# Edge stage of a graph network on one Trainium2 core: the lower parts of the normalised rows computed on GpSimd, the first sums waiting for them by fifths, and the remainders of the later edge weights moved to later rounds

## The chip, the core and the metric

The kernel runs on 1 core of one Trainium2 chip. The core has five engines with a queue each: TensorE (PE, matmuls; PEld are its weight loads), VectorE (DVE), ScalarE (ACT), GpSimd (POOL) and SyncE (SP, which only starts DMAs here). They meet through semaphores. The metric is the device time of one execution in microseconds: 2258.76 us before the change, the median of 3 runs (2257.27 to 2259.66).

## The reference, cut to what matters

Two layers act on x of 3125 nodes by 256 features with 100000 edges sorted by destination. The stage that is changed computes the first neighbour sum and, in the same pass, the matrix of edge weights that the second layer needs:

```
xn    = layernorm(x)
neigh = segment_sum(xn[src], dst, n)          # the edge stage: sums of gathered rows
h     = (1 + eps) * xn + neigh                # and, beside it, A[src, dst] += edge_weight
h     = relu(h @ W1 + b1) @ W2 + b2           # two dense layers, run inside the edge stage
h     = batchnorm(h) * gamma + beta
x     = x + h + attention(xn)                 # then experts, a second graph layer, experts
```

## The kernel before, in words

The nodes are padded to T = 25 tiles of 128. The edges lie in 1564 windows; four windows make an octet (391 of them), two octets a batch of 8 windows. For a batch, VectorE writes three tiles in `hots_dve` (L1001, L1002, L1006): one-hot rows of the keys, one-hot rows of the low bits (`lo`), and the one-hot keys times the three bf16 parts of the edge weight. TensorE multiplies them in `hots_pe` (L1027, L1029, L1032) into a bank for each octet (banks 0 to 3 in turn). ScalarE copies each bank out twice in `hots_act` (L1048): the counts to `CNT` (in `WB`) and the weights to `AWB` (in `X`). The one-hot tiles have two buffers: VectorE's batch n waits until TensorE is through with batch n-2 (`win`). A bank is used again when ScalarE has emptied it (`wev`).

Eight batches make a round, b = 0 to 24, which fills 128 columns of the counts. In round b+1 TensorE also forms the sums of round b (`sums_pe`, L1088): 25 tiles of counts times the normalised rows, each as an upper part `xnh` and a lower part `xnl` (fp32r words), in eight pieces i = 0 to 7 of 3 or 4 tiles. Batches are done in pairs, so TensorE's order in a round is batches 0 and 1, pieces 0 and 1, batches 2 and 3, pieces 2 and 3, and so on. From round 3 the dense layers (L1130, L1140) run in between as well.

The two parts of the rows are made in round 0. ScalarE rounds the rows of five tiles (a fifth, 1280 columns) into `xnh` (L1200) behind its batches 1 to 5. VectorE subtracts, `xnl = xn - xnh`, in place over `XN` (L1226), behind its batches 3 to 7. The first piece of sums (b = 1, i = 0) waits for all five lower parts.

The weights of the edges are turned into columns by TensorE ahead of the stage and split into three bf16 parts: VectorE's remainders (`first_rest_dve` L432, `second_rest_dve` L440) and ScalarE's casts (`highs_act`, `mids_act` L436, `lows_act` L444). There are four groups f of 512 windows (the last has 28). Groups 0 and 1 are done before the stage, groups 2 and 3 in rounds 1 and 2. Group f is first read in round 8 f. The order of each engine is written out by hand: `count_dve`, `count_act`, `count_pe` and `count_pool` are loops over rounds and i. On GpSimd, `count_pool` reads a flag and opens the semaphore `gate`, for which `sums_dve` (L1113) of round 2 waits; from there until its first gather at 649 us GpSimd has nothing to do.

Of the kernel before, what the change touches and what calls it, by code (L numbers as in the profile page):

```python
# [5 lines left out]
F32 = mybir.dt.float32  # L6
# [3 lines left out]
ALU = mybir.AluOpType  # L10
# [6 lines left out]
T = 25  # L17
# [54 lines left out]
def program(nc, ctx, a, out):  # L72
    at, sems = {}, {}

    def S(name):
        if name not in sems:
            sems[name] = ctx.enter_context(nc.semaphore(name))
        return sems[name]
# [233 lines left out]
    def degrees_pool(e):  # L312
        e.wait_ge(S("fold"), 2 * WG)
        e.wait_ge(S("good"), 1)
        e.tensor_scalar(deg2, deg2, goodc, None, ALU.mult).then_inc(S("degrees"), 1)
        e.wait_ge(S("degrees"), 1)
        e.dma_start(DEG.rearrange("(g p r) -> p g r", g=WG, r=2), deg2).then_inc(S("deg_out"), 16)
# [39 lines left out]
    def twice(v):  # L357
        return v.unsqueeze(2).to_broadcast([128, v.shape[1], 2])
# [61 lines left out]
    def dve_step(f, k):  # L420
        return FILLS + 4 * (f // 2) + 2 * k + f % 2 + 1

    def act_step(f, k):
        return FILLS + 6 * (f // 2) + 2 * k + f % 2 + 1

    def rest_of(f):
        o = windows_of(f)
        return left[f][:, 0:o.stop - o.start]
# [5 lines left out]
    def mids_act(e, f):  # L434
        e.wait_ge(S("key16"), dve_step(f, 0))
        e.copy(parts2[f][:, :, 1, :], twice(rest_of(f))).then_inc(S("lo16"), 1)  # L436

    def second_rest_dve(e, f):
        e.wait_ge(S("lo16"), act_step(f, 1))
        e.tensor_tensor(rest_of(f), rest_of(f), parts2[f][:, :, 1, 0], ALU.subtract).then_inc(S("key16"), 1)  # L440

    def lows_act(e, f):
        e.wait_ge(S("key16"), dve_step(f, 1))
        e.copy(parts2[f][:, :, 2, :], twice(rest_of(f))).then_inc(S("lo16"), 1)  # L444
# [522 lines left out]
    xnh, xnl = hr_, XNr  # L967
# [82 lines left out]
    def octets_to(b):  # L1050
        return min(16 * (b + 1), OCTETS)
# [20 lines left out]
    def fifth(g):  # L1072
        return slice(g * 5 * D, (g + 1) * 5 * D)

    xn_all = XN[:, :, :].rearrange("p t d -> p (t d)")

    def sums_pe(e, b, i):
        bk = B[4 + b % 2]
        if i == 0:
            e.wait_ge(S("cev"), octets_to(b))  # L1080
            if b == 0:
                e.wait_ge(S("xmix"), PAIRS)
                e.wait_ge(S("xnl"), 5)
            if b >= 2:
                e.wait_ge(S("gadd"), b - 1)
        for h in range(T * i // 8, T * (i + 1) // 8):
            for x in (xnh, xnl):
                m = e.matmul(bk[:, 0:D], CNT[b % 2][:, h, :], x[:, h * D:(h + 1) * D],  # L1088
                             start=(h == 0 and x is xnh), stop=(h == T - 1 and x is xnl), skip_group_check=True)
        if i == 7:  # L1090
            m.then_inc(S("gmm"), 1)
# [73 lines left out]
    def has_batch(b, i):  # L1165
        return b < T and 8 * b + i < NB
# [24 lines left out]
    def count_act(e):  # L1191
        highs_act(e, 2)
        for b in range(T + 6):
            for i in range(8):
                if has_batch(b, i):
                    hots_act(e, 8 * b + i)
                if b == 0 and 1 <= i < 6:
                    if i == 1:
                        e.wait_ge(S("fold"), 2 * WG)
                    e.copy(xnh[:, fifth(i - 1)], xn_all[:, fifth(i - 1)]).then_inc(S("xnh"), 1)  # L1200
                if (b, i) == (0, 6):
                    highs_act(e, 3)
                if b == 1 and i in (2, 4):
                    mids_act(e, 1 + i // 2)
                if (b, i) in ((1, 6), (2, 0)):
                    lows_act(e, b + 1)
                if i == 0 and 2 <= b < T + 2:
                    sums_act(e, b - 2)
                if i == 1 and layers_at(b - 2) is not None:
                    layer2_act(e, layers_at(b - 2))  # L1210
                if i == 6 and layers_at(b) is not None:
                    layer1_act(e, layers_at(b), 0)
                if i == 1 and layers_at(b - 1) is not None:
                    layer1_act(e, layers_at(b - 1), 1)

    def count_dve(e, d):
        e.tensor_scalar(scalec, epsc, goodc, 1.0, ALU.mult, ALU.add).then_inc(S("xts"), 1)
        for b in range(T + 6):
            for i in range(8):
                if has_batch(b, i) and (b or i):  # L1220
                    hots_dve(e, 8 * b + i)
                if b == 0 and 3 <= i:
                    if i == 3:
                        e.wait_ge(S("xd_out"), 80)
                    e.wait_ge(S("xnh"), i - 2)
                    e.tensor_tensor(xnl[:, fifth(i - 3)], xn_all[:, fifth(i - 3)], xnh[:, fifth(i - 3)].bitcast(F32), ALU.subtract).then_inc(S("xnl"), 1)  # L1226
                if b == 1 and i in (1, 3):
                    first_rest_dve(e, 2 + i // 2)
                if b == 1 and i in (5, 7):
                    second_rest_dve(e, i // 2)  # L1230
                if i == 3 and 2 <= b < T + 2:
                    sums_dve(e, b - 2)
                if i == 6 and layers_at(b - 2) is not None:
                    stats_dve(e, layers_at(b - 2))
        e.wait_ge(S("bst"), 2 * PAIRED)
        for c in range(2):
            d.add(e.bn_aggr(bmv[:, c, :], bst[:, c, :, :]))
            d.wait()
            e.tensor_scalar(bsc[:, c, 0:1], bmv[:, c, 1:2], 1.0, 1e-5, ALU.mult, ALU.add).then_inc(S("bvar"), 1)
            e.wait_ge(S("bstd"), c + 1)  # L1240
            d.add(e.reciprocal(bsc[:, c, 0:1], bsc[:, c, 0:1]))
            d.wait()
            d.add(e.tensor_tensor(bsc[:, c, 0:1], bsc[:, c, 0:1], gac[:, c:c + 1], ALU.mult))
            d.wait()
            d.add(e.tensor_tensor(bsc[:, c, 1:2], bmv[:, c, 0:1], bsc[:, c, 0:1], ALU.mult))
            d.wait()
            e.tensor_tensor(bsc[:, c, 2:3], bec[:, c:c + 1], bsc[:, c, 1:2], ALU.subtract).then_inc(S("bscale"), 1)

    def count_pool(e):
        e.wait_ge(S("good"), 2)
# [1215 lines left out]
    def pool_program(e):  # L2470
        windows_pool(e)
        degrees_pool(e)
        count_pool(e)
        e.wait_ge(S("xd_out"), 160)
        e.wait_ge(S("fill"), 16 * NF)
        gather_pool(e, 0, 0)
        slots_pool(e, 0, lambda: e.wait_ge(S("y_out"), 80))
        between(e, iter(()), lambda i: None, lambda: gather_pool(e, 1, 0), lambda i: None)
        slots_pool(e, 1, lambda: wait_out(e))
# [82 lines left out]
    @block.gpsimd  # L2562
    def _(e):
        pool_program(e)
# [79 lines left out]
```

## Time and profile before

| | |
|---|---|
| time, median of 3 runs | 2258.76 us (2257.27 to 2259.66) |
| the profiled execution: its own time, its span | 2251.02 us, 2249.4 us |
| busy share of the span: PE, PEld, DVE, ACT, POOL | 93%, 87%, 74%, 55%, 25% |
| mean granted clock of TensorE | 0.969 |
| the edge stage: first one-hot tile of round 0; last sums | 141.4 us; 568.4 us |

The shares of busy time are over the whole span. The edge stage is the stretch from 141 to about 570 us, and the change touches its first 100 us. In the page's picture of 40 slices (56 us each) the slices from 112 to 168 us show PE at 9 tenths falling to 5 and DVE at 8. Timelines and windows show the same stretch closely. Times of single instructions overlap a little at their ends, so the cost of one in a full queue is the distance from its start to the next one's start.

### The profile page before, as it was taken

The numbers are of one execution on the slowest core, as the hardware profiler recorded it, in microseconds if no ns is written. First come the engines' busy times: TensorE is split into PE (matmuls) and PEld (weight loads), VectorE is DVE, ScalarE is ACT, GpSimd is POOL, SyncE is SP. The second block draws the span as 40 slices with busy tenths as digits, with TensorE's granted clock in tenths as the row PEclk, the third lists the DMA queues.
The fourth block names the chain that finished last, engine by engine and source line by source line (L and its number), as shares of the span: only waits on it lengthen the run. The fifth ranks groups of instructions, "written<-read, shape, count | busy, mean of one in ns | idle before, by whom it ended". The sixth has DMA issues, their size and how long they took to land. (4 is left out here: it accounts for less than half of the span.)

```text
span 2249.4 us, 47270 instructions
## 1 busy us (share of the span) xinstructions
PE 2094.8 (93%) x18287; PEld 1966.0 (87%) x18287; DVE 1659.0 (74%) x3119; ACT 1234.4 (55%) x2875; POOL 566.6 (25%) x406
## 2 busy tenths in 40 slices
PE   5559999999879999998999999999999999999996
PEld 3459999999779999997778999899988999999996
DVE  6888888886588888885656666556667867888885
ACT  5566555555537767764524444444435336667664
POOL 3100000000036777771000000000000014777775
PEclk9779999999889999999989999999999999999998
DMA  4414333334457777874002666366641026777776
GB/s 130 137 62 116 95 114 90 105 104 115 141 174 226 239 226 225 241 227 117 1 25 78 189 187 181 114 187 188 189 149 53 22 92 179 242 225 224 239 216 168
DMA packets 241114, 339.04 MB, mean 151 GB/s; under 512 B 33407, under 2 KB 202546, under 8 KB 240754
## 3 DMA queue, kind: packets, MB, share of 16 engines
q1 hardware_dynamic: 208908, 296.19, 41.7%
q0 software_dynamic: 28528, 35.76, 8.6%
q10 hardware_dynamic: 3446, 3.97, 0.6%
q8 instruction: 150, 2.46, 0.5%
q14 instruction: 82, 0.67, 0.1%
HBM read 258.89 MB, written 76.95 MB: 149 GB/s over the span
## 5 line engine op out<-in xcount | busy, mean ns | idle before, releaser
L1982 POOL DMA_INDIRECT SC<-xd,slot_i x128 | 183.4, 1433 | 1457.1 <-DVE slot_q L1618 1324.6
L2376 PE MATMUL bank<-WB_r,XN_r 128*128 128x448 f32 x1400 | 399.8, 367 | 3.7 <-DVE WB_r L2335 3.7
L2335 DVE TENSOR_TENSOR WB_r<-WB,WB_r 128x448 fp32r<-128x448 f32 x350 | 214.0, 625 | 166.1 <-ACT WB_r L2328 166.0
L2328 ACT CAST WB_r<-WB 128x448 fp32r<-128x448 f32 x350 | 197.6, 568 | 222.2 <-PE bank L2376 217.6
L2376 PEld LDWEIGHTS bank<-WB_r,XN_r 128*128 128x128 f32 x1400 | 263.2, 188 | 26.8 <-DVE wb__r L2301 4.4
L1912 PE MATMUL bank<-SC_r,WB_r 128*128 128x256 f32 (+1 forms) x2064 | 250.5, 280 | 9.7 <-issue 7.8
L1912 PEld LDWEIGHTS bank<-SC_r,WB_r 128*128 128x128 f32 x2064 | 243.9, 188 | 14.3 <-issue 14.1
L1048 ACT CAST WB_r<-bank 128x200 fp32r<-128x200 f32 x391 | 144.1, 369 | 165.2 <-PE bank L1032 164.3
L1927 PE MATMUL bank<-R_r,H_r 128*128 128x256 f32 x1752 | 216.1, 282 | 4.8 <-DVE R_r L1823 4.8
L1927 PEld LDWEIGHTS bank<-R_r,H_r 128*128 128x128 f32 x1752 | 209.9, 190 | 5.1 <-issue 5.1
L1775 ACT ACTIVATE wb_<-bank,WB 128x256 f32<-128x256 f32 (+1 forms) x344 | 133.5, 477 | 80.1 <-PE bank L1912 41.0
L1988 POOL DMA_INDIRECT slot_p<-pd,slot_q x128 | 158.4, 1237 | 63.6 <-issue 33.5
L1912 PE MATMUL bank<-SC_r,XN_r 128*128 128x256 f32 x1392 | 169.5, 280 | 4.5 <-issue 3.8
L1912 PEld LDWEIGHTS bank<-SC_r,XN_r 128*128 128x128 f32 x1392 | 164.8, 188 | 8.2 <-issue 8.1
L1784 ACT ACTIVATE yo<-yo,slot_p 128x256 f32<-128x256 f32 x118 | 53.7, 502 | 210.1 <-DVE yo L1862 205.6
L1088 PE MATMUL bank<-H_r,WB_r 128*128 128x256 f32 x625 | 165.7, 300 | 0.0
L2376 PE MATMUL bank<-WB_r,R_r 128*128 128x448 f32 x448 | 164.9, 368 | 0.0
L1088 PE MATMUL bank<-XN_r,WB_r 128*128 128x256 f32 x625 | 154.6, 282 | 0.0
L1048 ACT COPY X<-bank 128x200 f32<-128x200 f32 x391 | 148.0, 378 | 0.0
L1002 DVE TENSOR_TENSOR SC<-R,DR 128x1024 bf16<-128x1024 bf16 x196 | 134.3, 685 | 0.0
L1088 PEld LDWEIGHTS bank<-XN_r,WB_r 128*128 128x128 f32 x625 | 119.8, 192 | 0.1
L1088 PEld LDWEIGHTS bank<-H_r,WB_r 128*128 128x128 f32 x625 | 119.6, 191 | 0.1
(463 smaller groups left out, 5153.6 us busy)
## 6 DMA issues: line engine op xcount, KB each, us to landing
WB<-adjw SPq DMA_DIRECT2D x350, 224.0 KB, 2.9
WB<-in_f_pack SPq DMA_DIRECT2D x127, 512.0 KB, 6.1
WB<-in_f_pack SPq DMA_DIRECT2D x62, 640.0 KB
adjw<-X SPq DMA_DIRECT2D x24, 1600.0 KB, 7.8
WB<-in_f_pack SPq DMA_DIRECT2D x65, 516.0 KB
xd<-XN SPq DMA_DIRECT2D x15, 640.0 KB, 5.5
y<-X SPq DMA_DIRECT2D x10, 640.0 KB, 3.3
X<-y SPq DMA_DIRECT2D x6, 640.0 KB, 6.7
```

Of the source, the lines that this page charges most:

```text
L1002: e.tensor_tensor(by_two(hot_lo[s][:, 0:m, :]), row(iota16, o), along(lo2, o, 128), ALU.is_equal).then_inc(S("lo1"), 1)
L1048: e.copy(to[b % 2][:, :, 8 * j:8 * j + 8].rearrange("p h (q r) -> p q h r", r=2), bank[:, :, i]).then_inc(S(name), 1)
L1088: m = e.matmul(bk[:, 0:D], CNT[b % 2][:, h, :], x[:, h * D:(h + 1) * D], start=(h == 0 and x is xnh), stop=(h == T - 1 and x is xnl), skip ...
L1775: m = e.activation(st[:, q * w:(q + 1) * w], B[hp][:, q * TS:q * TS + w], gfun[L], bias=b[:, hc:hc + 1])
L1784: e.activation(ob[:, q, :], ob[:, q, :], ACT.Copy, scale=slot_p[:, 2 * i + q:2 * i + q + 1]).then_inc(S("obs"), 1)
L1912: m = e.matmul(B[hp][:, q * TS:q * TS + w], p[:, c * HID + hc * 128:c * HID + (hc + 1) * 128], x[:, c * w:(c + 1) * w], start=(c == 0 and ...
L1927: m = e.matmul(bk[:, s * D:(s + 1) * D], x[:, hc * w + s * 128:hc * w + (s + 1) * 128], p[:, hc * D:(hc + 1) * D], start=(hc == 0 and n == ...
L1982: e.indirect_dma_start(yin[i % 2][:, q * D:(q + 1) * D], None, XD, bass.IndirectOffsetOnAxis(ap=slot_i[:, 2 * i + q:2 * i + q + 1], axis=0 ...
L1988: e.indirect_dma_start(slot_p[:, 2 * i + q:2 * i + q + 1], None, PD.rearrange("(r k) -> r k", k=1), bass.IndirectOffsetOnAxis(ap=slot_q[:, ...
L2328: e.copy(split_w(m)[0], RAW[m % PR]).then_inc(S("whigh"), 1)
L2335: e.tensor_tensor(al, RAW[m % PR], ah.bitcast(F32), ALU.subtract).then_inc(S("wlow"), 1)
L2376: mm_ = e.matmul(conv_bank(k, band, c)[:, 0:PW], x[st][:, o], y, start=(st == 0 and i == 0), stop=(st == T - 1 and i == 2))
```

## The change

Four edits, on four engines.

- The subtraction `xnl = xn - xnh` of all five fifths goes from VectorE (L1226 before) to GpSimd, in a new function `lower_rows_pool`, ahead of `count_pool` in GpSimd's program.
- Piece i of the first sums waits for as many fifths as its tiles need (1, 2, 2, 3, 3, 4, 5, 5 for i = 0 to 7) and no longer for all five.
- VectorE's first remainders of groups 2 and 3 go from round 1 to round 2, and its second remainders from round 1 to the ends of rounds 4 and 5.
- ScalarE's casts of them go from rounds 1 and 2 to round 2 and rounds 5 and 6.

```diff
@@ sums_pe
             if b == 0:
                 e.wait_ge(S("xmix"), PAIRS)
-                e.wait_ge(S("xnl"), 5)
             if b >= 2:
                 e.wait_ge(S("gadd"), b - 1)
+        if b == 0:
+            e.wait_ge(S("xnl"), (T * (i + 1) // 8 - 1) // 5 + 1)
@@ count_act
-                if b == 1 and i in (2, 4):
-                    mids_act(e, 1 + i // 2)
-                if (b, i) in ((1, 6), (2, 0)):
-                    lows_act(e, b + 1)
+                if b == 2 and i in (4, 6):
+                    mids_act(e, i // 2)
+                if b in (5, 6) and i == 2:
+                    lows_act(e, b - 3)
@@ count_dve
-                if b == 0 and 3 <= i:
-                    if i == 3:
-                        e.wait_ge(S("xd_out"), 80)
-                    e.wait_ge(S("xnh"), i - 2)
-                    e.tensor_tensor(xnl[:, fifth(i - 3)], xn_all[:, fifth(i - 3)], xnh[:, fifth(i - 3)].bitcast(F32), ALU.subtract).then_inc(S("xnl"), 1)
-                if b == 1 and i in (1, 3):
+                if b == 2 and i in (1, 3):
                     first_rest_dve(e, 2 + i // 2)
-                if b == 1 and i in (5, 7):
-                    second_rest_dve(e, i // 2)
+                if b in (4, 5) and i == 7:
+                    second_rest_dve(e, b - 2)
@@ new
+    def lower_rows_pool(e):
+        e.wait_ge(S("xd_out"), 80)
+        for j in range(5):
+            e.wait_ge(S("xnh"), j + 1)
+            e.tensor_tensor(xnl[:, fifth(j)], xn_all[:, fifth(j)], xnh[:, fifth(j)].bitcast(F32), ALU.subtract).then_inc(S("xnl"), 1)
@@ pool_program
         degrees_pool(e)
+        lower_rows_pool(e)
         count_pool(e)
```

VectorE's queue in round 0 before, from the end of batch 3 on. A batch is the three rows L1001, L1002, L1006; L1226 is a lower part:

```order
L1002 TENSOR_TENSOR SC<-R,DR 128x1024
L1006 TENSOR_TENSOR SC<-SC,WB 128x8x150
L1226 TENSOR_TENSOR XN_r_51<-XN,H_r_49 128x1280
L1001 TENSOR_TENSOR wb_<-R,DR 128x8x50
L1002 TENSOR_TENSOR SC<-R,DR 128x1024
L1006 TENSOR_TENSOR wb_<-wb_,WB 128x8x150
L1226 TENSOR_TENSOR XN_r_51<-XN,H_r_49 128x1280
L1001 TENSOR_TENSOR SC<-R,DR 128x8x50
L1002 TENSOR_TENSOR SC<-R,DR 128x1024
L1006 TENSOR_TENSOR SC<-SC,WB 128x8x150
```

The same place now:

```order
L1002 TENSOR_TENSOR SC<-R,DR 128x1024
L1006 TENSOR_TENSOR SC<-SC,WB 128x8x150
L1001 TENSOR_TENSOR wb_<-R,DR 128x8x50
L1002 TENSOR_TENSOR SC<-R,DR 128x1024
L1006 TENSOR_TENSOR wb_<-wb_,WB 128x8x150
L1001 TENSOR_TENSOR SC<-R,DR 128x8x50
L1002 TENSOR_TENSOR SC<-R,DR 128x1024
L1006 TENSOR_TENSOR SC<-SC,WB 128x8x150
```

The five subtractions between the batches are gone from VectorE's queue; the batches stand one behind the other.

GpSimd's queue before, behind the sums of the edge weights (L315) and their store. `TENSOR_LOAD flagi` is the start of `count_pool`:

```order
L315 TENSOR_SCALAR small<-small 128x26 [waits good,fold]
L317 DMA deg<-small 128x13x2 [waits degrees]
L1255 TENSOR_LOAD flagi [waits good]
L1255 ISA x2
L1256 COMPARE_AND_BRANCH
```

The same place now:

```order
L315 TENSOR_SCALAR small<-small 128x26 [waits good,fold]
L317 DMA deg<-small 128x13x2 [waits degrees]
L1253 TENSOR_TENSOR XN_r_51<-XN,H_r_49 128x1280 [waits xnh,xd_out]
L1253 TENSOR_TENSOR XN_r_51<-XN,H_r_49 128x1280 [waits xnh] x4
L1257 TENSOR_LOAD flagi [waits good]
L1257 ISA x2
```

The five subtractions stand ahead of the flag, so the opening of `gate` now comes behind them.

## Rows read from the trace of the kernel before

**Rows 1.** Windows of the edge stage; columns as in its header line.

```profile
...
core 0: us, PE busy (x) PEld busy (x) DVE busy (x) ACT busy (x) POOL busy (x), PEclk, DMA share, GB/s
...
148.00:157.00 9.00, 5.50 (x96) 5.31 (x97) 8.75 (x14) 6.47 (x16) 0.00 (x0) 0.50 0.23 75
157.00:166.00 9.00, 4.65 (x84) 4.43 (x82) 9.00 (x13) 5.86 (x16) 0.00 (x0) 0.50 0.00 0
...
171.00:185.00 14.00, 13.21 (x235) 12.91 (x233) 12.87 (x26) 8.78 (x30) 0.00 (x0) 0.93 0.25 69
...
```

**Rows 2.** Waits between 142 and 171 us: total, times, longest.

```profile
...
PE bank L1027 <- DVE SC L1002: 9.9, 6, 2.4
PE bank L1027 <- DVE SC L1006: 4.9, 1, 4.9
...
DVE XN_r L1226 <- ACT H_r L1200: 0.2, 1, 0.2
```

**Rows 3.** Timeline of VectorE, round 0: start, duration, instruction.

```profile
...
151.98 0.78 DVE L1006 TENSOR_TENSOR SC<-SC,WB 128x1200 bf16<-128x1200 bf16 x1
152.91 1.49 DVE L1226 TENSOR_TENSOR XN_r<-XN,H_r 128x1280 fp32r<-128x1280 f32 x1 [0.15 <-ACT H_r L1200]
154.32 0.36 DVE L1001 TENSOR_TENSOR wb_<-R,DR 128x400 bf16<-128x400 bf16 x1
...
155.89 1.49 DVE L1226 TENSOR_TENSOR XN_r<-XN,H_r 128x1280 fp32r<-128x1280 f32 x1
...
168.67 0.78 DVE L1006 TENSOR_TENSOR SC<-SC,WB 128x1200 bf16<-128x1200 bf16 x1
...
```

**Rows 4.** Timeline of ScalarE, round 0.

```profile
...
152.70 0.35 ACT L1048 CAST WB_r<-bank 128x200 fp32r<-128x200 f32 x1
...
153.57 1.31 ACT L1200 CAST H_r<-XN 128x1280 fp32r<-128x1280 f32 x1
154.73 0.39 ACT L1048 CAST WB_r<-bank 128x200 fp32r<-128x200 f32 x1
...
```

**Rows 5.** Timeline of TensorE: one batch at 151 us, and the first sum.

```profile
...
151.11 0.24 PE L1027 MATMUL bank<-wb_,SC 128*128 128x100 bf16 x1
...
152.45 0.18 PE L1032 MATMUL bank<-R 128*128 128x8 bf16 x1
...
170.93 0.56 PE L1088 MATMUL bank<-H_r,WB_r 128*128 128x256 f32 x1
...
```

**Rows 6.** Lines L432 and L440: ns min/median/max, first and last start.

```profile
...
L432 DVE TENSOR_TENSOR WB<-bank,R x1: 847/847/847, 169.4 to 169.4; 128x512 f32<-128x512 f32 x1
L432 DVE TENSOR_TENSOR R<-bank,R x1: 180/180/180, 173.3 to 173.3; 128x28 f32<-128x28 f32 x1
...
L440 DVE TENSOR_TENSOR WB<-WB,R x1: 871/871/871, 177.5 to 177.5; 128x512 f32<-128x512 f32 x1
L440 DVE TENSOR_TENSOR R<-R x1: 199/199/199, 181.4 to 181.4; 128x28 f32<-128x28 f32 x1
...
```

**Rows 7.** Waits from 171 to 200 us, then from 200 to 540 us.

```profile
...
PE bank L1027 <- issue: 1.0, 3, 0.6
...
DVE wb_ L1001 <- PE bank L1032: 60.1, 72, 1.2
...
```

**Rows 8.** Timeline of GpSimd from 60 to 250 us.

```profile
...
108.09 0.37 POOL L315 TENSOR_SCALAR small<-small 128x26 f32<-128x26 f32 x1 [46.45 <-DVE flagi L390]
...
```

**Rows 9.** Timelines of GpSimd and VectorE at 749 us; VectorE's line L1823.

```profile
...
748.48 1.59 POOL L2012 DMA_INDIRECT y<-yo,slot_i  x1 [0.30 <-issue]
...
749.13 0.67 DVE L1851 CAST XT_r<-XT 128x512 fp32r<-128x512 f32 x1
...
750.44 0.42 DVE L1851 CAST XT_r<-XT 128x512 fp32r<-128x512 f32 x1
...
L1823 DVE TENSOR_TENSOR WB_r<-WB,WB_r x66: 1211/1220/1284, 648.6 to 2229.0; 128x1024 fp32r<-128x1024 f32 x66
...
```

**Rows 10.** Waits from 560 to 640 us, behind the edge stage.

```profile
...
DVE XT L1113 <- PE bank L1102: 18.0, 2, 10.5
...
```

## The prediction

> **What bounds the kernel now.** I read the windows of the edge stage first, then the waits, then the timelines of the four engines. From 148 to 166 us VectorE is busy for 17.75 of 18 us, TensorE for 10.15 at a granted clock of 0.50, its lower level of 1.2 GHz, and GpSimd for nothing [rows 1]. TensorE's waits from 142 to 171 us end on VectorE's one-hot tiles: 14.8 us in seven waits [rows 2]. So VectorE sets the pace of round 0. A batch costs it 1.57 us (154.32 to 155.89) and a lower part 1.41 (152.91 to 154.32) [rows 3]; in the whole stretch it waited for ScalarE's upper parts for 0.2 us [rows 2]. The first sum starts at 170.93 [rows 5], about 1.5 us behind the end of VectorE's batch 9 (168.67 + 0.78 [rows 3]). From there on TensorE is busy for 13.21 of 14 us and its clock rises (mean 0.93 from 171 to 185) [rows 1]. It lacks only 1.0 us until 200 us [rows 7]. After that VectorE waits for TensorE, 60.1 us in 72 waits up to 540 us [rows 7]: TensorE bounds the other rounds.
>
> So what counts is when TensorE gets its first sum and whether batches come fast enough in round 1. Everything behind moves with it. The end of the stage is a chain without slack, where VectorE waits 10.5 us in one piece for the turned sums [rows 10], so I carry a shift there to the end of the kernel in full.
>
> **The change part by part.** *Lower parts off VectorE.* Five instructions of 1.41 us leave round 0: 7.0 us. Batches 4 to 9 then need 6 x 1.57 = 9.4 us from 152.7 (behind batch 3), so batch 9 would be ready at 162.1 if VectorE ran as before.
>
> *ScalarE is late next.* The four copies of a batch take it 0.87 us (152.70 to 153.57) and an upper part 1.16 (153.57 to 154.73) [rows 4], 2.03 together, more than VectorE's 1.57. Three more such pairs behind 154.73 (batches 3 to 5) end at 160.8, batch 6 and a small cast at 161.8, and batch 7 begins to free banks at 162.2. TensorE's batch 9 waits for these banks and takes 1.5 us at the lower clock (151.11 to 152.63 [rows 5]). So with VectorE untouched by GpSimd the first sum comes at 163.7 to 163.9, 7.1 us earlier.
>
> *Lower parts on GpSimd.* No row has a GpSimd instruction with two inputs. GpSimd's only arithmetic in the stage is one TENSOR_SCALAR of 26 columns, 0.37 us [rows 8], where VectorE's subtraction of 28 columns takes 0.20 [rows 6]. By that ratio, 1.85, a fifth of 1.49 us on VectorE [rows 3] is 2.76 us on GpSimd; I take 2.8. From below it is bounded by VectorE's own 1.49. From above I take 3.7 (2.5 times, since the ratio of small instructions says little about long ones). Beside nothing else, fifths of 2.8 us end at 155.6, 158.4 and so on to 166.8, and the last is needed by piece 6, some 10 us behind the first sum (173.7); even 3.7 us (171.3) would be in time. The wait by fifths therefore costs nothing then; it saves waiting for the fifth that is last.
>
> *The Trainium skill prices it too.* Its page "GPSIMD Engine Reference", section "Elementwise — side-by-side cycle accounting", gives 1.96 times VectorE's time for a tensor_tensor add of fp32. By that a fifth would be 2.9 us; no row here shows it, and the sum would be 0.5 us higher.
>
> *What GpSimd does to VectorE.* Two rows bear on it, and they differ. A single-source cast of VectorE takes 0.42 us (750.44) but 0.67 while a GpSimd instruction runs beside it (749.13 within 748.48 + 1.59) [rows 9]: the two do get in each other's way. Subtractions of two inputs, 1024 columns, in the same stages stay at 1211 to 1284 ns in all 66 cases [rows 9], although GpSimd is at work there. But GpSimd's instructions there are gathers, which read one column of indices. The new ones stream two inputs of 1280 columns, as VectorE's do. I take it that the two engines then take turns at a path that they share, an instruction at a time. Under turns VectorE stands still for GpSimd's 5 x 2.8 = 14.0 us, all of it ahead of batch 9, because ScalarE hands over a fifth every 2.03 us and GpSimd is always asking. Batch 9 ends at 152.7 + 9.4 + 14.0 = 176.1, and the first sum follows 1.5 us later, at 177.6: 6.7 us later than 170.93.
>
> *The page that speaks against the change.* The Trainium skill, page "SBUF — State Buffer", section "Who interferes with whom", says that a VectorE instruction with two SBUF inputs contends with a GpSimd instruction that reads SBUF, and that the holder keeps the shared ports for its whole instruction. The stretched cast agrees with such a lock; no row shows it for two inputs.
>
> *Remainders moved.* Round 1 loses four remainders on VectorE, 0.85 + 0.18 + 0.87 + 0.20 = 2.1 us [rows 6], of which the two first ones go to round 2 and the second ones to rounds 4 and 5, where VectorE waits for TensorE 0.83 us at a time (60.1 / 72 [rows 7]) and hides them; two of them are 0.9 us. Their weights are not read before round 16. In round 1 this lets VectorE run ahead, and TensorE's 1.0 us without work until 200 us [rows 7] goes. If VectorE is still late in round 2, the two first ones have no cover there, cost up to 1.0 and eat this gain.
>
> *`gate`.* It opens behind the fifths, by about 175 us under turns. Its only user, L1113, stands in round 2, a whole round (some 14 us) behind the first sum, so it does not wait.
>
> *Sum.* Under turns: -7.0 off VectorE and +14.0 standing still, less 0.3 of small gaps that VectorE had before, is the +6.7 of the first sum; -1.0 in round 1 leaves +5.7. I take +5.5, as some of GpSimd's turns fall in waits of VectorE. On the profiled execution this gives 2251.0 + 5.5 = 2256.5 us. The median of the runs stands 7.7 us above that execution, so the forecast is 2258.8 + 5.5 = 2264.3 us. The ends of this case are 5 x 1.49 = 7.5 standing still, -1 in all, and 5 x 3.7 = 18.5, +10: 2258 to 2269.
>
> **Rivals.** *A: no contention.* VectorE keeps its pace as in the 66 subtractions. The first sum comes 7.1 us earlier, ScalarE sets it, and the 1.0 us of round 1 goes unless ScalarE or the low clock keeps it: -6.5 to -8, I take -7.1, 2251.7 us. For it: no two-input row is stretched. Against: those rows stand beside gathers alone. This is the side below the kernel before.
>
> *B: cheap turns or partial sharing.* GpSimd's instructions hold VectorE for less than their length, 1.4 to 2.2 us each. At 5 x 1.7 = 8.5 us what is lost equals what is saved with the 1.0 of round 1 (7.0 + 0.3 + 1.0 = 8.3). Between 1.4 and 2.2 the time moves by -1.3 to +2.7; 2259.5 us. It decides against the forecast if a GpSimd fifth beside VectorE costs VectorE under 2.5 us.
>
> *C: GpSimd starves.* VectorE's queue is full, so GpSimd gets the path only in VectorE's gaps. VectorE then has batch 9 at about 162, but the second fifth is not there and the wait moves to TensorE, at pieces 1 to 6 (L1089). The work to be done on the one path before piece 6 is the same 14.0 us, so the end is about that of the forecast: +5, 2263.8 us. It differs in place, not in time.
>
> *D: it does less than it says*, because ScalarE's upper parts hold the stage: VectorE alone would allow the first sum at 162.1 + 1.5 = 163.6 us and ScalarE at 163.7 to 163.9, so this takes 0.3 us at most and is in A.
>
> **How the numbers follow.** Turns with a full price, C among them, 0.53; B 0.20; A 0.27. Under 0.2% (4.5 us) a measurement of this kernel can't tell a change from none. Full turns are over it on the slow side in 0.46 of their 0.53 and else within; B is within; A is over it on the fast side in 0.26. Together faster 0.26, within 0.27, slower 0.47. The likeliest case alone ranges from 2258 to 2269. The range reaches down to A's 2251.7 less 0.7 and up to 2268.5: 2251.0 to 2268.5.
>
> **What the profile after would show.** For turns: L1001, L1002 or L1006 with about 3 us in five or so cases between 153 and 175 us against a usual 0.4 to 0.8; L1253 about 2.8 us, starting 2.8 to 3.5 us apart; the first L1089 near 177 us. For A: no VectorE instruction stretched, first L1089 near 164, clock up by 167. For C: TensorE waits that end on L1253. VectorE's remainders in rounds 2, 4 and 5 should have no wait of TensorE behind them. I am wrong if the first sum comes before 171 us.

## The result and the profile after

The changed kernel takes 2265.13 us (median of 11 runs, 2258.29 to 2267.38), against 2258.76 us before (11 runs, 2254.51 to 2263.09). The ratio is 1.0025 with a 95% interval of 1.0016 to 1.0035: slower by 5.7 us (3.6 to 7.9). The two medians themselves are 6.4 us apart.

The two profiled executions differ by more: spans of 2249.4 and 2260.6 us. 7.1 us of this is there before the change can act, at the first instruction of `count_dve` (L1217, now L1218): 147.7 us before, 154.8 after. There the code is the same; the first reader of the gathered edges (L322) starts at 64.4 us in the one and at 71.5 in the other, behind gathers of GpSimd whose last starts at 59.4 and 61.4. The ten other kernels profiled for this study fall into two groups that go with the chip, or with the time at which that chip was used: the four on one chip reach this instruction at 146 to 148 us, the six on two other chips at 154 to 156, and in both groups are kernels whose code ahead of the stage is that of before. The kernel before takes 2247.62 us on the first of these chips and 2257.85 and 2257.31 on the others. The first profiled execution of the kernel before, at 2251.02 us, lies below all 11 runs that its median rests on, so it may come from the quicker chip too; on which chip it ran isn't on record. So times in the stage are told from here on from the start of this instruction, and the comparison of whole kernels rests on the ratios.

In this measure the first sum came 23.2 us into the stage and comes at 29.7 now. The last addition of sums (L1113, now L1114) started at 422.9 us and now at 429.4. The whole loss of the stage, 6.5 us, arises ahead of the first sum and is then carried unchanged to its end. Behind the stage this pair of executions differs by 2.4 us the other way, less than single executions of one kernel scatter. The lines of the changed kernel that show both ends are these two (ns min/median/max, first and last start):

```profile
...
L1089 PE MATMUL bank<-H_r,WB_r x625: 278/283/562, 184.5 to 581.8; 128*128 128x256 f32 x157
...
```

```profile
...
L1114 DVE SCALAR_TENSOR_TENSOR XT<-XT,cols,bank x25: 331/478/481, 201.9 to 584.2; 128x256 f32<-128x256 f32 x24, 128x112 f32<-128x112 f32 x1
...
```

The windows of the changed kernel's stage, to set beside [rows 1] (mind the 7.1 us):

```profile
...
core 0: us, PE busy (x) PEld busy (x) DVE busy (x) ACT busy (x) POOL busy (x), PEclk, DMA share, GB/s
...
157.00:166.00 9.00, 5.75 (x101) 5.44 (x99) 8.91 (x9) 7.16 (x18) 5.91 (x2) 0.50 0.09 28
166.00:171.00 5.00, 0.00 (x0) 0.00 (x0) 5.00 (x3) 1.54 (x3) 5.00 (x3) 0.50 0.00 0
171.00:178.00 7.00, 3.83 (x67) 3.72 (x68) 6.91 (x9) 3.11 (x10) 2.91 (x2) 0.50 0.00 0
184.50:198.50 14.00, 13.81 (x250) 13.56 (x247) 12.00 (x23) 7.27 (x31) 0.00 (x0) 0.92 0.22 60
...
```

From 166 to 171 us TensorE does nothing at all and GpSimd is busy throughout. The granted clock of TensorE is 0.50 up to 178 us. In the 14 us behind the first sum it is 0.92 on the mean, as it was before (0.93 from 171 to 185 [rows 1]): the clock rises at the same place behind the first sum in both kernels and is no part of the loss. What TensorE waits for from 142 to 178 us is told badly by the list of waits. Its largest item names no engine but "issue", since a stretched instruction of VectorE shows as busy, not as late:

```profile
...
PE bank L1027 <- issue: 11.3, 4, 8.1
...
```

The timeline of GpSimd has four subtractions back to back and the fifth behind ScalarE's last upper part:

```profile
...
160.09 13.07 POOL L1253 TENSOR_TENSOR XN_r<-XN,H_r 128x1280 fp32r<-128x1280 f32 x4 [42.92 <-ACT H_r L1201]
177.25 2.91 POOL L1253 TENSOR_TENSOR XN_r<-XN,H_r 128x1280 fp32r<-128x1280 f32 x1 [4.09 <-ACT H_r L1201]
```

VectorE's timeline beside it (start, duration, instruction):

```profile
...
159.80 0.36 DVE L1001 TENSOR_TENSOR wb_<-R,DR 128x400 bf16<-128x400 bf16 x1
160.08 0.68 DVE L1002 TENSOR_TENSOR SC<-R,DR 128x1024 bf16<-128x1024 bf16 x1
160.68 3.48 DVE L1006 TENSOR_TENSOR wb_<-wb_,WB 128x1200 bf16<-128x1200 bf16 x1
164.08 3.05 DVE L1001 TENSOR_TENSOR SC<-R,DR 128x400 bf16<-128x400 bf16 x1
167.05 3.37 DVE L1002 TENSOR_TENSOR SC<-R,DR 128x1024 bf16<-128x1024 bf16 x1
170.34 3.45 DVE L1006 TENSOR_TENSOR SC<-SC,WB 128x1200 bf16<-128x1200 bf16 x1
173.72 0.36 DVE L1001 TENSOR_TENSOR wb_<-R,DR 128x400 bf16<-128x400 bf16 x1
...
177.04 0.37 DVE L1001 TENSOR_TENSOR wb_<-R,DR 128x400 bf16<-128x400 bf16 x1
177.32 3.38 DVE L1002 TENSOR_TENSOR SC<-R,DR 128x1024 bf16<-128x1024 bf16 x1
...
```

Here the mechanism can be read row by row. L1002 at 160.08 started ahead of GpSimd and takes its usual 0.68 us. Then L1006 takes 3.48 us instead of 0.78, L1001 3.05 instead of 0.36, L1002 3.37 instead of 0.68, L1006 3.45 instead of 0.78: each is its own length plus 2.67 to 2.70 us. Between two GpSimd instructions exactly one of VectorE gets through. From 173.72 on the tiles are normal again, since GpSimd waits for ScalarE, which itself waits for TensorE; the fifth subtraction then holds one more tile, at 177.32. Five holds make 13.4 us. GpSimd's own records are longer than the holds (2.9 to 3.4 us). The longer ones hold their wait for their turn; a subtraction that waits for nothing takes 2.89 us (two early fifths on GpSimd, below), 0.2 more than it holds:

```profile
...
L1253 POOL TENSOR_TENSOR XN_r<-XN,H_r x5: 2908/3325/3432, 160.1 to 177.2; 128x1280 fp32r<-128x1280 f32 x5
...
```

### The profile page after: what moved, and what is told of

It reads as the page before. It is cut to its first block and busy times, and to the rows that moved or that the text cites. A ratio compares the mean times of both kernels' runs of the same rounds, so it can differ in the third digit from the quotient of the medians.

```text
span 2260.6 us, 47270 instructions
## 1 busy us (share of the span) xinstructions
PE 2091.8 (93%) x18287; PEld 1959.9 (87%) x18287; DVE 1664.6 (74%) x3114; ACT 1233.9 (55%) x2875; POOL 582.1 (26%) x411
## 5 line engine op out<-in xcount | busy, mean ns | idle before, releaser
L1984 POOL DMA_INDIRECT SC<-xd,slot_i x128 | 177.6, 1387 | 1394.4 <-DVE slot_q L1620 1261.6
L1990 POOL DMA_INDIRECT slot_p<-pd,slot_q x128 | 165.3, 1292 | 63.6 <-issue 36.3
L1089 PE MATMUL bank<-H_r,WB_r 128*128 128x256 f32 x625 | 165.9, 301 | 0.0
L1089 PE MATMUL bank<-XN_r,WB_r 128*128 128x256 f32 x625 | 154.8, 282 | 0.0
L1002 DVE TENSOR_TENSOR SC<-R,DR 128x1024 bf16<-128x1024 bf16 x196 | 139.3, 711 | 0.0
L1089 PEld LDWEIGHTS bank<-XN_r,WB_r 128*128 128x128 f32 x625 | 120.0, 192 | 0.1
L1089 PEld LDWEIGHTS bank<-H_r,WB_r 128*128 128x128 f32 x625 | 119.7, 192 | 0.1
```

Of the source, the lines that this page charges most:

```text
L1002: e.tensor_tensor(by_two(hot_lo[s][:, 0:m, :]), row(iota16, o), along(lo2, o, 128), ALU.is_equal).then_inc(S("lo1"), 1)
L1984: e.indirect_dma_start(yin[i % 2][:, q * D:(q + 1) * D], None, XD, bass.IndirectOffsetOnAxis(ap=slot_i[:, 2 * i + q:2 * i + q + 1], axis=0 ...
L1990: e.indirect_dma_start(slot_p[:, 2 * i + q:2 * i + q + 1], None, PD.rearrange("(r k) -> r k", k=1), bass.IndirectOffsetOnAxis(ap=slot_q[:, ...
```

## The experiments

All times "into the stage" are from profiled executions and are counted from the start of L1217 or L1218. Ratios are to the kernel before on the same chip, with 95% intervals; the column of the kernel before shows that the chips differ by 10 us, so times of different chips are not to be set side by side. The last two rows are single executions.

| kernel | first sum | last addition | time, us | before, us | ratio |
|---|---|---|---|---|---|
| before | 23.2 | 422.9 | | | 1 |
| changed | 29.7 | 429.4 | 2265.13 | 2258.76 | 1.0025 [1.0016, 1.0035] |
| GpSimd part alone | 29.7 | 429.5 | 2262.28 | 2257.85 | 1.0020 [1.0010, 1.0030] |
| moved remainders alone | 23.3 | 422.9 | 2256.32 | 2257.85 | 1.0000 [0.9991, 1.0010] |
| no lower parts | 16.8 | 415.7 | 2261.74 | 2257.85 | 1.0018 [1.0009, 1.0027] |
| ten halves | 29.1 | 427.8 | 2261.61 | 2257.85 | 1.0017 [1.0009, 1.0026] |
| lower parts spread on VectorE | 18.7 | 420.6 | 2245.64 | 2247.62 | 0.9989 [0.9980, 0.9997] |
| the same, early upper parts | 18.6 | 420.3 | 2244.30 | 2247.62 | 0.9991 [0.9981, 1.0001] |
| two early fifths on GpSimd | 17.2 | 419.3 | 2244.26 | 2247.62 | 0.9983 [0.9974, 0.9992] |
| five early fifths on GpSimd | 25.3 | 424.0 | 2259.27 | 2257.31 | 1.0010 [1.0001, 1.0018] |
| idle instructions, one a round | 23.3 | 422.9 | 2249.25 | 2247.62 | |
| idle instructions in rows | 23.3 | 429.8 | 2266.43 | 2257.31 | |

The theory is that of the prediction: VectorE and GpSimd take turns, an instruction at a time, at a path for reading that instructions with two streams from SBUF need. Its rivals are that the moved remainders cost the time, that the two share the path piece by piece, and that any GpSimd instruction holds VectorE.

**GpSimd part alone.** The changed kernel with the remainders where they were.

```diff
-                if b == 2 and i in (1, 3):
+                if b == 1 and i in (1, 3):
                     first_rest_dve(e, 2 + i // 2)
-                if b in (4, 5) and i == 7:
-                    second_rest_dve(e, b - 2)
+                if b == 1 and i in (5, 7):
+                    second_rest_dve(e, i // 2)
```

> The changed kernel with the remainders of groups 2 and 3 back in round 1. Turns (VectorE stands still for each whole GpSimd subtraction, 5 x 2.7 us): the five long VectorE instructions stay, the first sum stays about 6.4 us late, and the time is 5.5 to 7.5 us over the kernel before (ratio 1.0024 to 1.0033), 0 to 1 us over the changed kernel. Rival (the moved remainders cost the time): back to the kernel before, ratio 1.000, with the first sum no more than 2 us late.

The ratio is 1.0020, and both marks in the stage are within 0.1 us of the changed kernel. VectorE's timeline of this kernel has the same long tiles:

```profile
...
160.64 3.48 DVE L1006 TENSOR_TENSOR wb_<-wb_,WB 128x1200 bf16<-128x1200 bf16 x1
164.04 3.05 DVE L1001 TENSOR_TENSOR SC<-R,DR 128x400 bf16<-128x400 bf16 x1
167.01 3.37 DVE L1002 TENSOR_TENSOR SC<-R,DR 128x1024 bf16<-128x1024 bf16 x1
...
```

So the GpSimd part makes the whole loss, and the moved remainders take nothing and give nothing that the marks or the interval of some 2 us either way can show.

**Moved remainders alone.** The kernel before with that half of the change.

```diff
-                if b == 1 and i in (1, 3):
+                if b == 2 and i in (1, 3):
                     first_rest_dve(e, 2 + i // 2)
```

(and the second remainders and ScalarE's casts as in the change)

> The kernel before with only the remainders moved to the later rounds; lower parts stay on VectorE and the sums wait for all five. Turns: 0.5 to 1 us faster than before (ratio 0.9995), TensorE's 1.0 us without work in round 1 gone, no VectorE instruction longer than before. Rival (the moved remainders cost the time): 4 to 6 us slower, ratio 1.002.

The ratio is 1.0000 and the marks are those of before. I had expected 0.5 to 1 us. The windows of its rounds 1 and 2, where the first sum starts at 179.5 us:

```profile
...
179.40:193.50 14.10, 13.91 (x253) 13.66 (x251) 12.17 (x23) 7.42 (x31) 0.00 (x0) 0.92 0.31 89
193.50:208.50 15.00, 14.30 (x280) 14.00 (x276) 14.49 (x30) 10.08 (x40) 0.00 (x0) 1.00 0.44 124
...
```

TensorE is busy for 13.91 of 14.1 us in round 1, as expected. But in round 2 it lacks 0.7 of 15. The kernel before has it the other way about: it lacks 0.8 in round 1 [rows 1] and 0.2 in the next 15 us:

```profile
...
185.00:200.00 15.00, 14.79 (x295) 14.50 (x292) 14.33 (x28) 9.71 (x41) 0.00 (x0) 1.00 0.50 143
```

The work without cover went with the remainders, from one round to the next.

**No lower parts.** What the stage would do with the five subtractions gone from every engine. The sums use the upper part twice, the second time into an unused half of the bank, so the lower parts are left out of the neighbour sums.

```diff
-            for x in (xnh, xnl):
-                m = e.matmul(bk[:, 0:D], CNT[b % 2][:, h, :], x[:, h * D:(h + 1) * D],
+            for k in range(2):
+                m = e.matmul(bk[:, k * D:(k + 1) * D], CNT[b % 2][:, h, :], xnh[:, h * D:(h + 1) * D],
```

> The changed kernel without the five subtractions on any engine: the second matmul of each pair in the sums takes the upper part again and writes a half of the bank that nothing reads, so the lower parts are left out of the neighbour sums. At its end the SyncE queue also waits for its last weight loads. Turns: no VectorE instruction is stretched, the first sum comes 7 us earlier than before, paced by ScalarE, and the time is 6.5 to 8 us under the kernel before (ratio 0.9965 to 0.997), 12 to 14 under the changed one. Rival (VectorE was not what held the stage, ScalarE or TensorE's low clock was): 0 to 3 us under the kernel before.

In the stage it went as expected: the first sum comes 6.4 us earlier than before and the last addition 7.2 us. The line of its sums (ns min/median/max, first and last start; the stage of this execution begins at 155.5 us):

```profile
...
L1089 PE MATMUL bank<-H_r,WB_r x1250: 277/283/562, 172.3 to 569.0; 128*128 128x256 f32 x179
...
```

The time did not follow, at 1.0018. In the groups of its profile (busy us, mean ns of one, idle time ahead) one line points to the cause:

```profile
...
L2014 POOL DMA_INDIRECT out<-yo,slot_i x62 | 103.5, 1670 | 47.1 <-ACT yo L1786 27.5 <-issue 15.6 <-DMA out<-yo,slot_i 4.0
...
```

The result scatter of the last expert layer has 62 instructions, against 60 in the kernel before. The likely reason, which no run shows, is that with other sums some tokens go to other experts and more tiles of expert work are done. Its last gather starts 46.6 us ahead of the end of the span, against 33.4 before. So the time of this kernel says nothing of the edge stage, and its marks do. The step to a time was a mistake in the design: a kernel that leaves work out must not change what later work there is.

**Ten halves.** Each subtraction cut into two of 640 columns.

```diff
+            for q in range(2):
+                o = slice((10 * j + 5 * q) * 128, (10 * j + 5 * q + 5) * 128)
+                e.tensor_tensor(xnl[:, o], xn_all[:, o], xnh[:, o].bitcast(F32), ALU.subtract).then_inc(S("xnl"), 1)
```

> The changed kernel with each GpSimd subtraction cut into two of 640 columns. Turns, an instruction at a time: about ten VectorE instructions of 1.3 to 1.5 us more than usual, 13 to 14 us in sum, and the time within 1.5 us of the changed kernel (ratio to before 1.002 to 1.003). Rival (a fixed price of each meeting of the two engines, about 2.7 us): up to 27 us standing still and 10 us slower. Rival (the path is shared element by element): no single long instructions, many small stretches.

VectorE's timeline has ten long tiles from 160 to 179 us, of which three are:

```profile
...
160.34 2.12 DVE L1006 TENSOR_TENSOR wb_<-wb_,WB 128x1200 bf16<-128x1200 bf16 x1
162.39 1.71 DVE L1001 TENSOR_TENSOR SC<-R,DR 128x400 bf16<-128x400 bf16 x1
164.02 2.02 DVE L1002 TENSOR_TENSOR SC<-R,DR 128x1024 bf16<-128x1024 bf16 x1
...
```

Each is 1.33 to 1.35 us over its usual length, so ten make 13.4 us, the sum of five at 2.7. The hold goes by GpSimd's columns and not by the meeting. The first sum comes 0.6 us earlier than in the changed kernel, and the ratio of 1.0017 lies within its interval.

The last addition comes 1.6 us earlier, 1.0 more than the first sum. What differs is TensorE's clock. In the kernel before and in the changed one the first 2 us of sums run at a granted clock of about 0.50; here TensorE is busy at 0.50 for 1.95 of the 2 us from 179.5 already, the clock rises from 181.5 on, and the first sums run at 1.00. The changed kernel, then this one (windows from the first sum):

```profile
...
184.50:186.50 2.00, 2.00 (x13) 2.00 (x10) 1.80 (x4) 0.58 (x3) 0.00 (x0) 0.50 0.77 220
...
```

```profile
...
183.50:185.50 2.00, 2.00 (x33) 1.96 (x29) 2.00 (x4) 0.82 (x4) 0.00 (x0) 1.00 1.01 290
...
```

From the first sum to the first addition it is 17.4 us in the kernel before and the changed one and 16.4 here. 2 us of work at half the clock account for the 1.0 us.

**What kind of GpSimd instruction holds.** The kernel before with idle GpSimd instructions of 720 columns on an unused part of `WB`.

```diff
+            if kind == 0:
+                m = e.memset(o, 0.0)
+            elif kind == 1:
+                m = e.tensor_copy(o, a)
+            else:
+                m = e.tensor_tensor(o, a, b, ALU.subtract)
+            m.then_inc(S("xnl"), 1)
```

A first run had one such instruction a round, at `gmm`.

> The kernel before, with twelve idle GpSimd instructions of 720 columns in rounds 9 to 20 of the edge stage, one a round, four times in turn a memset (writes alone), a copy (one input) and a subtraction (two inputs), on a part of WB that nothing uses then. It tells which GpSimd instructions hold VectorE's two-input tiles. Turns at a path that is for reading: the memsets stretch no VectorE instruction, the copies by about their own length (0.7 to 1 us), the subtractions by 1.5 us. Rival (any GpSimd instruction holds it): the memsets too. Rival (only two-input instructions do): the copies not. The time stays within 2 us of before.

It missed its aim on VectorE's side. Each instruction fell on the end of a tile and the wait behind it. The copies took 1.11 to 1.25 us, each begun while the tile L1006 had 0.5 to 0.6 us to run (one copy holds for 0.6, as the next run shows), the memsets 0.69 to 0.70. Only the subtractions reached VectorE's next tile, which took 0.62 or 0.76 us instead of 0.37. The stage kept its 422.9 us, and the time was 1.6 us over the median before. So a second run put them in rows.

> The kernel before with idle GpSimd instructions of 720 columns in rows, each row long enough to meet VectorE's starts: eight memsets (0.7 us each) from round 9, six copies (0.7) from round 12, four subtractions (1.7) from round 15. Turns at the reading side: while the memsets run no VectorE tile is longer than its usual 0.37, 0.69 or 0.78 us; the copies add up to 0.7 us to tiles that start beside them, the subtractions up to 1.7. Rival (writes hold it too): tiles beside the memsets are longer by up to 0.7. Rival (only two-input instructions hold it): tiles beside the copies keep their usual length.

GpSimd's timeline, eight memsets, six copies and four subtractions:

```profile
...
320.19 5.99 POOL L1263 MEMSET WB<- 128x720 f32 x8 [201.99 <-PE bank L1089]
370.12 6.30 POOL L1265 COPY WB<-WB 128x720 f32<-128x720 f32 x6 [43.94 <-PE bank L1089]
422.12 8.16 POOL L1267 TENSOR_TENSOR WB<-WB 128x720 f32<-128x720 f32 x4 [45.70 <-PE bank L1089]
```

VectorE beside the memsets:

```profile
...
321.83 0.37 DVE L1001 TENSOR_TENSOR wb_<-R,DR 128x400 bf16<-128x400 bf16 x1 [1.17 <-PE bank L1032]
322.11 0.68 DVE L1002 TENSOR_TENSOR SC<-R,DR 128x1024 bf16<-128x1024 bf16 x1
322.71 0.78 DVE L1006 TENSOR_TENSOR wb_<-wb_,R 128x1200 bf16<-128x1200 bf16 x1
...
```

beside the copies:

```profile
...
372.36 1.27 DVE L1002 TENSOR_TENSOR SC<-R,DR 128x1024 bf16<-128x1024 bf16 x1
373.55 1.36 DVE L1006 TENSOR_TENSOR wb_<-wb_,R 128x1200 bf16<-128x1200 bf16 x1
374.83 0.94 DVE L1001 TENSOR_TENSOR SC<-R,DR 128x400 bf16<-128x400 bf16 x1
...
```

beside the subtractions:

```profile
...
424.29 2.21 DVE L1002 TENSOR_TENSOR SC<-R,DR 128x1024 bf16<-128x1024 bf16 x1
426.42 2.29 DVE L1006 TENSOR_TENSOR wb_<-wb_,R 128x1200 bf16<-128x1200 bf16 x1
428.64 1.87 DVE L1001 TENSOR_TENSOR SC<-R,DR 128x400 bf16<-128x400 bf16 x1
...
```

Beside memsets the tiles keep 0.37, 0.68 and 0.78 us. Beside copies they are longer by 0.58 to 0.59, beside subtractions by 1.51 to 1.53. So what holds VectorE is that GpSimd reads from SBUF, with one input as with two, and not that it writes or is busy. Both rivals fall. The holds of the two rows add up to some 7.5 us, and this kernel's last addition came at 429.8 us, 6.9 later than before: in rounds where VectorE waits for TensorE by 0.8 us at a time [rows 7], rows of holds are hardly hidden.

**Lower parts spread on VectorE.** No GpSimd. The wait by fifths and the moved remainders as in the change; VectorE makes two fifths in round 0 and three in round 1.

```diff
+    LOWER_AT = ((0, 4), (0, 6), (1, 1), (1, 3), (1, 5))
-                if b == 0 and 3 <= i:
+                if (b, i) in LOWER_AT:
```

> The kernel before with the sums waiting by fifths, the remainders moved, and the five lower parts still on VectorE: two in round 0 (behind batches 4 and 6), three in round 1 (behind batches 9, 11 and 13). GpSimd does nothing. Turns (the loss of the changed kernel came from GpSimd alone, and the wait by fifths is worth what VectorE can defer): first sum about 4 us earlier than before, last sum 2 to 4 us earlier, ratio 0.9982 to 0.999. Rival (round 1 is bound by VectorE, so that what is deferred is paid there in full): last sum within 1 us of before, ratio 1.000.

The first sum comes 4.5 us earlier and the last addition 2.3. The rest is given back in round 1, where TensorE now waits on VectorE's stream of tiles in small pieces. Its waits of this kind from the first sum (164.7 us) to 200 us (total, times, longest), against 1.0 us in three before [rows 7]:

```profile
...
PE bank L1027 <- issue: 3.4, 7, 0.6
```

Since its clock is 1.00 from the first sum on (the ten halves show what that is worth), round 1 loses more to VectorE than the 2.2 us between the two marks.

**The same with early upper parts.** ScalarE makes `xnh` ahead of its batch 1, where it waited for 5.1 us.

```diff
+                if b == 0 and i == 0:
+                    for g in range(1, 5):
+                        e.copy(xnh[:, fifth(g)], xn_all[:, fifth(g)]).then_inc(S("xnh"), 1)
```

> As the version with the lower parts spread on VectorE, and ScalarE's upper parts all made ahead of its batch 1, where it waits for TensorE for 5.1 us; lower parts behind batches 3 and 5 and in round 1. Turns: VectorE is the bound of round 0, so it is within 1 us of the version without the early upper parts (last sum 2 to 4 us earlier than before). Rival (ScalarE holds round 0 once VectorE is relieved): 1 to 2 us faster than that version.

Within 0.3 us of the version without them in the stage, and the same in time. ScalarE did not hold round 0 at this pace of VectorE.

**Two early fifths on GpSimd.** With `xnh` early, GpSimd can read while VectorE's instructions take one of their streams from PSUM. VectorE does the other three fifths in round 1.

```diff
+        for j in range(2):
+            e.wait_ge(S("xnh"), j + 1)
+            e.tensor_tensor(xnl[:, fifth(j)], xn_all[:, fifth(j)], xnh[:, fifth(j)].bitcast(F32), ALU.subtract).then_inc(S("xnl"), 1)
```

> Early upper parts on ScalarE, the first two lower parts on GpSimd while VectorE still works from PSUM banks (its instructions there have one SBUF tensor input), three on VectorE in round 1, remainders moved. Turns, and only between instructions that both read two streams: GpSimd's first fifth stretches no VectorE instruction, its second one at most by the 1 to 2.7 us that reach into the one-hot batches; first sum 5.5 to 7 us and last sum 4 to 6 us earlier than before, ratio 0.9975 to 0.998. Rival (GpSimd blocks every VectorE instruction): VectorE's PSUM instructions are stretched by 2.7 us twice and the time is within 2 us of the version with early upper parts alone.

GpSimd's two subtractions, from 142.11 to 147.86 us:

```profile
...
142.11 5.75 POOL L1266 TENSOR_TENSOR XN_r<-XN,H_r 128x1280 fp32r<-128x1280 f32 x2 [33.37 <-ACT H_r L1198]
```

and VectorE beside them:

```profile
...
142.58 0.69 DVE L946 TENSOR_TENSOR X<-X,bank 128x512 f32<-128x512 f32 x1
143.18 0.88 DVE L943 SCALAR_TENSOR_TENSOR bank<-bank,small,rows 128x256 f32<-128x256 f32 x2
144.09 0.69 DVE L946 TENSOR_TENSOR X<-X,bank 128x512 f32<-128x512 f32 x1
...
146.07 2.02 DVE L1001 TENSOR_TENSOR SC<-R,DR 128x400 bf16<-128x400 bf16 x1
148.01 0.68 DVE L1002 TENSOR_TENSOR SC<-R,DR 128x1024 bf16<-128x1024 bf16 x1
...
```

L943 (0.88 us for two) and L946 (0.69), which read a bank and one stream from SBUF, keep their lengths. The first tile of two SBUF streams, L1001 at 146.07, takes 2.02 us instead of 0.36 and ends 0.2 us behind GpSimd's last subtraction (147.86). The price of two fifths is 1.7 us where VectorE would have paid 2.8. The first sum comes 6.0 us earlier than before and the last addition 3.6, a little under the 4 to 6 expected, for the same reason as above: round 1 is short of VectorE. At a ratio of 0.9983 this version is faster than both kernels. Against the version with early upper parts alone only the marks tell it apart (1.4 and 1.0 us earlier); the two times, 2244.26 and 2244.30 us, do not, so what excludes the rival here is the unchanged length of L943 and L946 and not the time. The run leaves one thing tied together: the tiles that were held are bf16 with two SBUF streams, those that were spared are fp32 with a PSUM bank as one of their streams.

**Five early fifths on GpSimd.** The changed kernel, its five subtractions moved ahead by the early upper parts. Cut from the edit are the waits ahead of the first copy.

```diff
+        e.copy(xnh[:, fifth(0)], xn_all[:, fifth(0)]).then_inc(S("xnh"), 1)
...
-                if b == 0 and 1 <= i < 6:
-                    if i == 1:
-                        e.wait_ge(S("fold"), 2 * WG)
-                    e.copy(xnh[:, fifth(i - 1)], xn_all[:, fifth(i - 1)]).then_inc(S("xnh"), 1)
+                if b == 0 and i == 0:
+                    for g in range(1, 5):
+                        e.copy(xnh[:, fifth(g)], xn_all[:, fifth(g)]).then_inc(S("xnh"), 1)
```

> The changed kernel with ScalarE's upper parts made early, so that GpSimd's five subtractions (2.7 us each) start about 13 us before they do now and run back to back from there. Turns: the first one and most of the second lie beside VectorE's PSUM instructions and cost nothing, about 9.7 us of holds are left instead of 13.5; first sum 0 to 2.5 us later than before against 6.4 in the changed kernel, last sum -1 to +2.5 us, ratio to before 0.9995 to 1.001. Rival (each GpSimd subtraction costs VectorE its 2.7 us wherever it stands): as the changed kernel, 1.002 to 1.003.

GpSimd's timeline:

```profile
...
151.60 15.39 POOL L1257 TENSOR_TENSOR XN_r<-XN,H_r 128x1280 fp32r<-128x1280 f32 x5 [33.63 <-ACT H_r L1198]
```

and VectorE's beside it:

```profile
...
155.57 2.00 DVE L1001 TENSOR_TENSOR SC<-R,DR 128x400 bf16<-128x400 bf16 x1
157.50 3.36 DVE L1002 TENSOR_TENSOR SC<-R,DR 128x1024 bf16<-128x1024 bf16 x1
160.79 3.45 DVE L1006 TENSOR_TENSOR SC<-SC,WB 128x1200 bf16<-128x1200 bf16 x1
164.16 3.05 DVE L1001 TENSOR_TENSOR wb_<-R,DR 128x400 bf16<-128x400 bf16 x1
...
```

The first subtraction costs nothing and the second 1.6 us; three more cost 2.7 each: 9.7 us instead of 13.4. First sum 2.1 us later than before, last addition 1.1, ratio 1.0010. The 1.0 us between the two marks is the clock again: it is 1.00 from the first sum on, as in the ten halves. A subtraction on GpSimd has no fixed price; the price depends on what VectorE runs beside it.

## Why the prediction was right, step by step

*The bound.* VectorE paced round 0. Right: with the five lower parts gone from all engines the first sum comes 6.4 us earlier (7.1 was worked out), and the last addition 7.2. The 0.8 us between them arise in round 1, whose first 2 us run at a clock of 0.87 there. The clock, which the prediction read but gave no term, is worth up to 1.0 us in this stage; in the changed kernel it is the same as before, so the forecast did not suffer.

*Turns.* Right, and in the form that was chosen between two rows that differed [rows 9]. The 66 subtractions stay short beside the gathers although GpSimd works, and the stretched cast was the better guide. It was a weak one: two casts just ahead of it, at 746.91 and 747.99 us, start beside the gather of 746.55 to 748.18 and keep 0.43 and 0.42 us, so to rest on the one stretched cast was in part luck:

```profile
...
746.91 0.43 DVE L1851 CAST XT_r<-XT 128x512 fp32r<-128x512 f32 x1 [1.83 <-ACT XT L1775]
...
747.99 0.42 DVE L1851 CAST XT_r<-XT 128x512 fp32r<-128x512 f32 x1
...
```

Why gathers spare two-input instructions was not tried; the memsets show that GpSimd may write without holding them.

*The price of a fifth.* 2.8 us was taken from a ratio of two small instructions [rows 6, 8]; 2.7 us was held, five times, 13.4 us for 14.0. A ratio of small instructions need not hold for long ones, so this came out well with some luck. The Trainium skill's figure ("GPSIMD Engine Reference", "Elementwise — side-by-side cycle accounting") of 1.96 times VectorE's time lies close by: 2.7 us held for 1.41 is 1.9.

*The first sum.* 6.7 us later was worked out, 6.4 to 6.5 measured. Four holds fell ahead of batch 6 and the fifth on batch 8, all ahead of batch 9, as said. GpSimd was not always asking, though: it waited 4.1 us for ScalarE's last upper part, which was itself late through the holds. The forecast that the first L1089 would stand near 177 us counted from the execution before; in the one shown it is 184.5, and less the 7.1 us that lie ahead of the stage 177.4.

*The moved remainders.* Wrong: "TensorE's 1.0 us without work until 200 us goes" was worth 0.0 us. The other sentence of that step, that the two first remainders have no cover in round 2 and eat the gain, is what happens: in the kernel with the moves alone TensorE lacks 0.2 us in round 1 and 0.7 in round 2. The term was mis-sized because what one round gained was counted (up to 1.0 us) and what the other lost was left as an "if".

*The sum.* The stage is 6.5 us longer and the kernel 5.7 (3.6 to 7.9 by the interval), for 5.5 predicted. The two errors, 0.6 us too much in the holds and 1.0 in the remainders, partly cancelled. Set beside the stage the forecast is 1.0 us short, so that 5.5 and 5.7 lie so close is in part luck.

*The rivals.* A is excluded by the long tiles. B asked for less than 2.5 us a fifth. C, a GpSimd that starves, is excluded by the alternation: VectorE's full queue gets one instruction between two of GpSimd. The Trainium skill, page "SBUF — State Buffer", section "Who interferes with whom", has this rule with both its exceptions, a GpSimd instruction that only writes and a VectorE instruction with at most one SBUF input, outside the modes in which it uses both of its ports; the tiles beside the memsets and the lengths of L943 and L946 agree with them. How many microseconds one hold lasts is seen only here. D, that ScalarE comes next as the bound, was not settled: without the lower parts TensorE waits for a bank of ScalarE for 0.9 us. The wait by fifths had nothing to do here, since the last fifth was ready (180.2 us) ahead of the first sum (184.5); its worth was seen where VectorE keeps the fifths.

*What stays open.* Whether a VectorE instruction with one SBUF stream is ever held beside a GpSimd instruction that reads was not tried; nor whether an fp32 instruction of VectorE with two SBUF streams is held as the bf16 ones are. That the edges arrive some 7 us later on two of the chips is seen; why is not.

## What to carry to other kernels

Work handed from VectorE to an idle GpSimd is not free: while VectorE runs instructions with two SBUF streams (bf16 ones here), each GpSimd instruction that reads SBUF stops it for nearly that instruction's whole length (2.7 us of 2.9), and GpSimd is slower at the same work. Put such work beside VectorE instructions that read PSUM and at most one SBUF stream, or give GpSimd what only writes. Before work is moved to a later round, look which round has VectorE time to spare: three fifths deferred to round 1 gave back half of what they had gained. And compare two executions from the same instruction on the same chip: two chips gave the kernel before 10 us apart.

## What the runs showed of the hardware

- A GpSimd subtraction of 1280 fp32 columns holds a bf16 VectorE tile with two SBUF streams for 2.67 to 2.70 us, one of 640 for 1.33 to 1.35, one of 720 for 1.5; VectorE does 1280 in 1.41.
- A GpSimd copy of 720 columns holds it for 0.58 to 0.59 us; a memset of 720 (0.7 us) does not.
- It works both ways: a GpSimd copy that meets a tile of VectorE takes 1.11 to 1.25 us.
- VectorE instructions of fp32 that read a PSUM bank and one SBUF stream are not held (0.69 us and 0.88 us for two, beside GpSimd as without).
- The first 2 us of the sums at a granted clock of 0.50 instead of 1.00 cost 1.0 us (17.4 us for 16.4 from first sum to first addition).
- The kernel before takes 2247.62 us on one chip and 2257.31 and 2257.85 on two others; some 8 us of this are there at the first instruction of `count_dve` already.
- A held instruction shows as a long busy one, not as a wait; the sign is a maximum in a line's min/median/max far over the median (L1001: 0.36 median, 3.05 at most).
